# Turning x1 for the GRU from 32x32 blocks on VectorE, and loading the other relations' weights one by one

## What is computed

```python
x = _layernorm(x + _L0_gnn_ref(x, adj, W, a_src, a_dst))        # graph attention, 4 heads -> x1
def _L1_gnn_ref(x, adj, weight, w_ih, w_hh, b_ih, b_hh):
    A = (adj != 0).astype(x.dtype)
    h = x                                                       # first state = x1
    for i in range(3):
        m = jnp.einsum('bnd,de->bne', h, weight[i])
        aggr = jnp.einsum('bst,bsd->btd', A, m)
        h = _gru_cell(aggr, h, w_ih, w_hh, b_ih, b_hh)
    return h
x = _layernorm(x + _L1_gnn_ref(x, adj, ...))                    # -> x2
x = _layernorm(x + _L2_gnn_ref(x, adj, ...))                    # 4 relations; adj holds only 0 and 1 here
x = _layernorm(x + _L3_gnn_ref(x, adj, W, a))                   # graph attention, 1 head
```

## Time and profile before

| | |
|---|---|
| runs (3) | median 2617.78 us, 2617.44 to 2618.26 |
| profiled execution, first to last instruction | 2616.2 us |
| busy: PE / PEld / DVE / ACT / POOL | 98% / 85% / 79% / 62% / 42% |
| granted TensorE clock, mean | 0.992 |
| data moved by DMA | 128.99 MB, 265105 packets, 49 GB/s |
| packets under 512 B | 139760 |

### The profile page before, as it was taken

One profiled execution on the slowest core, in us unless ns is written; L12 is line 12 of the kernel. 1 busy time (PEld: TensorE's weight loads), 2 busy tenths in 40 slices (PEclk: granted clock), 3 DMA queues, 4 the chain that ended last, 5 costly groups with the idle time before them and its releaser, 6 DMA issues.

```text
span 2616.2 us, 48544 instructions
## 1 busy us (share of the span) xinstructions
PE 2564.6 (98%) x14979; PEld 2219.6 (85%) x14979; DVE 2064.6 (79%) x5210; ACT 1629.9 (62%) x4153; POOL 1093.8 (42%) x1264
## 2 busy tenths in 40 slices
PE   7999999999999999999999999999999999999995
PEld 6888888888888888888888888888888888888884
DVE  7877887877887877887877887877887877887765
ACT  5556665666665666665666665666665666665553
POOL 1333444443444443444443444443444443444342
PEclk9999999999999999999999999999999999999997
DMA  5212121112121212111212121212121212121000
GB/s 166 78 39 54 33 52 46 52 50 58 32 53 44 54 50 58 32 53 43 54 50 58 31 54 42 55 50 58 31 54 42 55 49 58 31 55 38 27 13 21
DMA packets 265105, 128.99 MB, mean 49 GB/s; under 512 B 139760, under 2 KB 249840, under 8 KB 264816
## 3 DMA queue, kind: packets, MB, share of 16 engines
q1 hardware_dynamic: 245120, 107.97, 15.8%
q10 hardware_dynamic: 19696, 17.44, 2.0%
HBM read 108.27 MB, written 17.08 MB: 48 GB/s over the span
## 4 chain that ended last, share of the span: by engine, by line
PE 94%; DVE 1%; issue 1%; ACT 0%; POOL 0%; POOLq 0%; DVEq 0%; ACTq 0%
PE psum L938 60%; PE psum L792 10%; PE psum L926 6%; PE psum L853 6%; PE psum L975 3%; PE psum L842 3%; PE psum L869 2%; PE psum L811 1%; PE psum L913 1%; PE psum L861 1%; DVE stats L1351 0%; ACT x L1176 0%; POOL rstd L1508 0%; DVE first_scores L1322 0%; DVE moments L1355 0%
## 5 line engine op out<-in xcount | busy, mean ns | idle before, releaser
L938 PE MATMUL psum<-ag_h,wc_h 128*128 128x512 f32 (+1 forms) x1188 | 489.0, 412 | 2.7 <-issue 2.0
L938 PE MATMUL psum<-ht_h,whh_h 128*128 128x512 f32 (+1 forms) x1188 | 483.0, 407 | 0.7 <-ACT g_z L1159 0.6
L938 PE MATMUL psum<-ht_h,whh_l 128*128 128x512 f32 (+1 forms) x1188 | 462.8, 390 | 0.0
L938 PE MATMUL psum<-ag_l,wc_h 128*128 128x512 f32 (+1 forms) x1188 | 461.9, 389 | 0.0
L938 PE MATMUL psum<-ht_l,whh_h 128*128 128x512 f32 (+1 forms) x1188 | 461.7, 389 | 0.0
L938 PE MATMUL psum<-ag_h,wc_l 128*128 128x512 f32 (+1 forms) x1188 | 461.5, 388 | 0.0
L1506 POOL TENSOR_SCALAR rstd<-moments 128x2 f32<-128x2 f32 x256 | 73.3, 286 | 858.6 <-DVE moments L1355 854.1
L1557 POOL TENSOR_TENSOR ht<-ht,g_n 128x512 f32<-128x512 f32 (+1 forms) x198 | 251.7, 1271 | 71.3 <-ACT g_n L1164 63.7
L938 PEld LDWEIGHTS psum<-ht_h,whh_l 128*128 128x128 f32 x1188 | 224.9, 189 | 50.8
L938 PEld LDWEIGHTS psum<-ag_h,wc_l 128*128 128x128 f32 x1188 | 223.4, 188 | 50.5
L938 PEld LDWEIGHTS psum<-ht_l,whh_h 128*128 128x128 f32 x1188 | 225.7, 190 | 40.0
(11 more groups left out here) (152 smaller groups left out, 6218.3 us busy)
## 6 DMA issues: line engine op xcount, KB each, us to landing
first_scores<-first_kept SPq DMA_DIRECT2D x116, 256.0 KB, 3.7
adj_i<-in_adj_dram SPq DMA_DIRECT2D x128, 128.0 KB, 3.2
x_in<-in_x_dram SPq DMA_DIRECT2D x64, 256.0 KB, 3.8
out_dram<-out_t ACTq DMA_DIRECT2D x64, 256.0 KB, 2.5
x_blocks<-in_x_dram SPq DMA_DIRECT2D x464, 32.0 KB, 2.1
part<-in_adj_dram SPq DMA_DIRECT2D x32, 256.0 KB, 3.3
adj_g<-in_adj_dram SPq DMA_DIRECT2D x31, 256.0 KB, 3.3
last_scores<-last_kept SPq DMA_DIRECT2D x59, 128.0 KB, 3.0
```

Of the source, the lines that this page charges most:

```text
L938: last = mm(dst, s, m, start=(first and k == 0), stop=(last_part and k == len(flat) - 1))
```

## The change

Units from 5 on (halves 3 to 32) no longer use `gru_turn0`. SP writes x1 of the unit to a DRAM scratch (`x1_keep`), waits for its landing, reads it back in 32x32 blocks (`x1_blocks`, 4 DMAs of 512 pieces of 128 bytes; the blocked loads of x take the same new form), DVE transposes the blocks into `ht` (`x1_turn`), ACT rounds to `ht_h`, and DVE writes `ht_l` (`x1_low`). No bank of LIGHT is taken. The DVE transpose waits until both `gru_fin` steps of half k-2 have been through PE. The weights of further relations are no longer loaded at the start, but one by one by SP under the branch.

```diff
 SLOTS: "xs": 2 -> "xs": 4
-gru_agg(0,1,0)
-gru_agg(0,1,1)  att_pv(pre,1,1)  att_exp(pre,1,1)  gru_new(-1,2,1)  att_res(pre,1,1)
+gru_agg(0,1,0)  x1_keep(1,0)
+gru_agg(0,1,1)  x1_blocks(1,0)  att_pv(pre,1,1)  att_exp(pre,1,1)  gru_new(-1,2,1)  att_res(pre,1,1)
 gru_hn(0,1,0)
-gru_rzh(0,1,0)  gru_fin(-1,0)  att_norm(pre,1,1)  rel_bias(-1,0)
-gru_r(0,1,0)
-gru_z(0,1,0)  att_scores(post,-2,1,0)  rel_adjt(-1,0)  rel_mask(-1,0)
+gru_rzh(0,1,0)  gru_fin(-1,0)  att_norm(pre,1,1)  rel_bias(-1,0)  x1_keep(1,1)
+gru_r(0,1,0)  x1_turn(1,0)
+gru_z(0,1,0)  x1_blocks(1,1)  x1_low(1,0)  att_scores(post,-2,1,0)  rel_adjt(-1,0)  rel_mask(-1,0)
 gru_in(0,1,0)  gru_fin(-1,1)  gru_norm(-1,0)  att_prob(post,-2,1)  post_load(-1,1)
-gru_hn(0,1,1)  gru_turn0(1,0)
+gru_hn(0,1,1)
 gru_rzh(0,1,1)  att_xt(pre,2,0)  gru_n(0,1,0)  rel_h1(-1,0)  x_blocks(2,1)  rel_bias(-1,1)  att_norm(post,-2,0)
-        gru_new(0,1,0)  att_pt(post,-2,1,0)
-gru_r(0,1,1)  att_wh(pre,2,0,0)  att_wh(pre,2,0,1)  att_rows(pre,2,0)  rel_y1(-1,0)  gru_norm(-1,1)  gru_turn0(1,1)
+        gru_new(0,1,0)  att_pt(post,-2,1,0)  x1_turn(1,1)
+gru_r(0,1,1)  att_wh(pre,2,0,0)  att_wh(pre,2,0,1)  att_rows(pre,2,0)  rel_y1(-1,0)  gru_norm(-1,1)  x1_low(1,1)
         rel_rest(-1,0)
...
 SP:
+            def load_blocks(i, blocks):
+                for f in range(P // TURN):
+                    sp.dma_start(xs[i][f * TURN:(f + 1) * TURN].rearrange("i c (m j) -> i c m j", j=TURN),
+                                 blocks[f].rearrange("i c g b j -> i c (g b) j")).then_inc(s_xs[i], 16)
+            def x1_keep(u):
+                sp.wait_ge(s_x1, u + 1)
+                if u - 2 >= X1_BLOCKED:
+                    sp.wait_ge(s_ht0, u)
+                at = 2 * place_of(u)
+                sp.dma_start(x1_kept[u % 2].rearrange("g n d -> n g d"), x1[half_of(u) % 3][:, at:at + 2, :]).then_inc(s_x1_kept, 16)
+            def x1_blocks(u):
+                i = take(sp, "xs", "x1_blocks", u)
+                sp.wait_ge(s_x1_kept, 16 * (u - X1_BLOCKED + 1))
+                load_blocks(i, x1_kept[u % 2].rearrange("g (b i) (c f j) -> f i c g b j", i=TURN, f=P // TURN, j=TURN))
-                sp.dma_start(wrs[:], L2_gnn_weight[1:R].rearrange("r (c p) o -> p r c o", p=P)).then_inc(s_rest, 16)
+            def rel_rest(u):
+                with sp.If(any_other > 0):
+                    for r in range(2, R + 1):
+                        after(sp, s_yr_ps, (R - 1) * u + r - 2)
+                        sp.dma_start(wr_other[:], L2_gnn_weight[r - 1].rearrange("(c p) o -> p c o", p=P)).then_inc(s_wr, 16)
...
 ACT:
+            def x1_turn(u):
+                k = half_of(u)
+                act.wait_ge(s_ht0, u + 2)
+                f(ht_h[k % 2][:, :, unit_columns(u)], ht[k % 2][:, :, unit_columns(u)], ACT.Copy).then_inc(s_ht0_h, 1)
...
 DVE:
+            def x1_turn(u):
+                k = half_of(u)
+                i, rounds = ring("xs", "x1_blocks", u)
+                dve.wait_ge(s_fin_ps, 2 * k - 3)
+                dve.wait_ge(s_xs[i], 64 * (rounds + 1))
+                stand(dve)
+                nc.vector.transpose(ht[k % 2][:, :, unit_columns(u)], xs[i][:]).then_inc(s_ht0, 1)
+            def x1_low(u):
+                k = half_of(u)
+                dve.wait_ge(s_ht0_h, u + 2)
+                tt(ht_l[k % 2][:, :, unit_columns(u)], ht[k % 2][:, :, unit_columns(u)],
+                   ht_h[k % 2][:, :, unit_columns(u)].bitcast(F32), ALU.subtract).then_inc(s_ht0_l, 1)
```

More of the change, by code:

```diff
@@ L42 @@
     "att_xt": ("xt",), "x_blocks": ("xs",), "att_direct": ("light",),
-    "att_pt": ("light",), "att_pv": ("light",),
+    "x1_blocks": ("xs",), "att_pt": ("light",), "att_pv": ("light",),
     "rel_adjt": ("light", "adjt"), "rel_bias": ("x2s",), "rel_mask": ("mt",),
@@ L290, in placed @@
     if name == "x_blocks" and not blocked("pre", u):
+        return []
+    if name in ("x1_keep", "x1_blocks", "x1_turn", "x1_low") and u < X1_BLOCKED:
         return []
@@ L398, in bass_gnn_stack @@
         xt_h, xt_l = sb("xt_h", [P, C, 2 * P], F32R), sb("xt_l", [P, C, 2 * P], F32R)
-        wh = [sb(f"wh{i}", [P, 2, D + 2 * H0]) for i in range(2)]
+        wh = [sb(f"wh{i}", [P, 2, D + 2 * H0]) for i in range(SLOTS["wh"])]
         stats = [sb(f"stats{i}", [P, 2, 6]) for i in range(4)]
@@ L418, in bass_gnn_stack @@
         Y_OF = {"pre": 0, "post": 1}
+        x1_kept = [nc.dram_tensor(f"x1_kept{i}", (2, P, D), F32, kind="Internal").ap() for i in range(2)]
+        s_x1_kept = sem("x1_kept_landed")
         class Layer:
@@ L463, in bass_gnn_stack @@
         s_x = [sem(f"x_loaded{i}") for i in range(2)]
-        s_xs, s_xturned = [sem(f"x_blocks_loaded{i}") for i in range(2)], sem("x_turned")
+        s_xs, s_xturned = [sem(f"x_blocks_loaded{i}") for i in range(SLOTS["xs"])], sem("x_turned")
         s_adj = [sem(f"adj_loaded{i}") for i in range(2)]
@@ L671, in pre_load @@
                 sp.dma_start(x_in[i][:], x[2 * u:2 * u + 2].rearrange("g n d -> n g d")).then_inc(s_x[i], 16)
+            def load_blocks(i, blocks):
[12 more added lines that the diff above has]
+                load_blocks(i, x1_kept[u % 2].rearrange("g (b i) (c f j) -> f i c g b j", i=TURN, f=P // TURN, j=TURN))
             def x_blocks(u):
                 i = take(sp, "xs", "x_blocks", u)
[L675 to L678, removed]
+                load_blocks(i, x[2 * u:2 * u + 2].rearrange("g (b i) (c f j) -> f i c g b j", i=TURN, f=P // TURN, j=TURN))
             def gru_load(k):
@@ L945, in gru_hn @@
                         pe.wait_ge(s_prep_lo, len(PIECES))
-                    pe.wait_ge(s_ht0_l, 2 * k + 2)
+                    pe.wait_ge(s_ht0_l, 2 * k + (2 if k < half_of(X1_BLOCKED) else len(units(k))))
                 else:
@@ L1195, in _ @@
                        "rel_adjt": rel_adjt, "rel_h1": rel_h1, "rel_rest": rel_rest,
-                       "gru_turn0": gru_turn0, "gru_agg": gru_agg, "gru_hn": gru_hn, "gru_r": gru_r, "gru_z": gru_z,
+                       "x1_turn": x1_turn, "gru_turn0": gru_turn0, "gru_agg": gru_agg, "gru_hn": gru_hn, "gru_r": gru_r, "gru_z": gru_z,
                        "gru_n": gru_n, "gru_turn": gru_turn, "rel_norm": rel_norm, "gru_norm": gru_norm})
@@ L1468, in _ @@
                        "att_res": att_res, "att_norm": att_norm, "rel_h1": rel_h1, "rel_y1": rel_y1,
-                       "rel_rest": rel_rest, "gru_turn0": gru_turn0,
+                       "rel_rest": rel_rest, "x1_turn": x1_turn, "x1_low": x1_low, "gru_turn0": gru_turn0,
                        "gru_agg": gru_agg, "gru_z": gru_z, "gru_in": gru_in, "gru_new": gru_new, "gru_split": gru_split,
```

30 lines of the change are left out of this document (20 added, 10 removed).

## The result

The changed kernel takes **2795.68 us** (median of 4 runs, 2793.32 to 2796.65) against 2618.02 us for the kernel before beside it (2617.44 to 2622.21). The ratio is 1.0676, with an interval of 1.0661 to 1.0691: slower by 6.8%. The forecast was 2753 us, with a range of 2660 to 2805. Its direction and both stops were right; it was 43 us short. The forecast's own range for the case of two stops, 2725 to 2790, does not hold the measured time; the wide range does, because it also took in most of the rival "the blocks land late" (2782 to 2817).

The account below looks back on a forecast made before the run. PE was taken as the bound, never waiting. Two new stops, less the transposes shed, cost 4.6 us in each of 29 halves (133.4), plus 2.0 and 1.6 on 2616.2: 2753 us, range 2660 to 2805.

Parts of the forecast that it names:

- the case of two stops: PE stands before `rel_h1` and again before `att_pv`: 3.9 to 5.8 us a half, 2725 to 2790 us; chance 0.66.
- the blocks land late: Rival: scratch blocks reach DVE's first turn 1 to 2.2 us later, shifting everything behind: 2782 to 2817 us; chance 0.12.
- The bound and the gain: PE never waits and sets the time; removing 236 transposes at 0.44 us per four saves 26.0 us.
- Which stop comes first, and who stands behind the wait: DVE's first turn waits, holding ACT, then POOL's mask; PE stands 2.46 us before `rel_h1`.
- What ends the wait: PE's transposes of `gru_fin(-1,1)`, done at 1307.34, release DVE's first turn; the blocks' landing is hidden.
- I take the early half: Of block landings between 1306.1 and 1309.6 the early half was taken; the late end adds 2.2 us.
- The second stop: PE stands 3.0 us before `att_pv` for the bank freed by ACT's `wh` copy; both stops make 4.6 us a half.
- PE alone sets the rest of the half.: Behind `att_pv` PE has its old work, helpers at most some 1.5 us later; nothing is made good or added.
- The other edits: Relation weights: one load fewer at the start, an untaken SP branch per unit; -2 to +1 us, taken as nothing.
- The sum: 29 halves x 4.6 = 133.4, plus 2.0 for half 32, on 2616.2, plus 1.6: 2753 us, 5.2% slower.
- PE only sheds its work: Rival: the mask is ready when PE comes, so only the 26.0 us go: 2592 us; chance 0.09.
- only the first stop holds: Rival: POOL or DVE makes up time, so the bank for `att_pv` is free: +46, 2664 us; chance 0.09.

Follow-up runs that it names:

- e9: Changed kernel with the first turn behind the `wh` copies, the second at the half's end, SP's second-unit store and loads behind `post_load(-1,1)`: 2594.11 us, 0.9913 of before.
- e5: e3 with PE turning both units of the finished half back in the half's first `gru_fin`: 2728.48 us, ratio 1.0423 to before.
- e6: e3 with SP's store of the first unit (`x1_keep(1,0)`) issued one line earlier: 2713.53 us, ratio 1.0366 to before.
- e4: Changed kernel with 23 identity transposes on PE put in each of the two stops, results overwritten: 2774.2 us, ratio 1.0599 to before.
- e7: Changed kernel without the scratch path: PE's `gru_turn0` as before, but one-by-one relation weights and four-DMA input blocks kept: 2616.41 us, ratio 0.9993 to before.
- e3: Changed kernel with only the second turn of a half moved, behind the `wh` copies: 2728.61 us, ratio 1.0423 to before.

## Why the prediction was right, and where its sum was short

- **The bound and the gain.** Right. PE alone set the time, and of its 26.0 us all but 2.6 came back in e9, where nothing waits.
- **Which stop comes first, and who stands behind the wait.** Right on the place and on the queues: DVE stands before the transpose, ACT behind DVE, POOL's `rel_bias` and mask behind ACT, and PE before `rel_h1`, released by POOL's mask. The stop was forecast at 2.46 us and is 2.65 (79.4 / 30). From the transpose's start to `rel_h1` the sum had 1313.84 - 1307.45 = 6.39 us; the rows above have 1312.75 - 1306.43 = 6.32.
- **What ends the wait.** Wrong: the forecast had PE end it, and the landing did in all 30 halves. The term that failed is the way through DRAM ("I take the early half"), and it makes 0.74 us a half (21 us). The store went 7.34 us ahead of the end of PE's transposes by the forecast and 7.14 in the trace. The forecast then counted 2.5 (landing of the store) + 1.5 (three issues more) + 2.1 (landing) = 6.1 us; the chain shows 3.28 + 2.02 + 2.33, and with the hand-overs 1306.43 - 1298.62 = 7.81. The largest miss is the store's landing, 0.8 us, for which the forecast gave no bounds; the issues are 0.5 more, the blocks' landing 0.2 and the hand-overs 0.2. The issues (bounds 1.5 and 2.9) and the blocks' landing (2.1 and 4.2) did fall nearer their early ends. The rival "the blocks land late" named the view that decides this, and that view decided for it. Its price of 1 to 2.2 us a half was too high for the 0.74 found, so that the measured time lies inside its 2782 to 2817 only because the clock, which it did not count, added about as much. e5 and e6 show which wait is last, and e6 that with the other one the forecast's 6.50 us hold. The Trainium skill, DMA: Bandwidth & Descriptors, Specifications, had been quoted for pieces under 512 bytes running below line rate. No run here shows whether that bears on the landing, for all the loads of blocks have pieces of 128 bytes: 64 KB of them land in 2.4 us, 32 KB in 2.1.
- **The second stop.** Right in cause and releaser: ACT's `wh` copy behind the second turn. Its end was forecast 8.41 us behind `rel_h1` and came at 8.41 in 10 of 27 halves and at about 8.17 in the others; that it meets the forecast exactly is chance. The forecast's path ran over POOL's L1614, and that is the path in the halves with 8.17 us. In the 10 others the clock is low while `rel_h1` runs, its result comes late, and DVE is still at the two L1406 on `out_t` when L1614 is done (the rows above: 1316.13 + 1.52 = 1317.65 against 1315.88 + 1.30 = 1317.18); the sum had neither. PE's idle time there is 1.9 us a time (48.5 / 26), not 3.0, mostly because its own work between the stops ran at half clock in many halves, so that PE came later. Idle time and lost time are two things here.
- **"PE alone sets the rest of the half."** Right on the waits, wrong on the pace, because the sum had no term for the clock. Between 180 and 2480 us the clock falls to 0.5 for 3.4 us 27 times, once in each half. In 16 of them it falls between 0.7 us before and 1.3 us behind the start of `rel_h1`. The work slowed there lies ahead of the second stop, which waits for ACT and swallows the loss but for 0.24 us (8.41 against 8.17). In the other 11 it falls some 9 us behind `rel_h1`, on work of the third part, and that part is then 69.9 instead of 68.33 us. That is 0.66 us a half in the third part and, against e4, 0.09 in the second, 22 us in all; e4 puts it at 21.5 us in the kernel's whole time. The other 0.13 us of the third part stays in e4 (68.34 against the forecast's 68.21), so it isn't the clock; its cause is open. No rival had the clock either.
- **The other edits.** Right: e7 shows no cost.
- **The sum.** 2753 + 29 x (0.74 + 0.79 - 0.16) = 2793; measured 2795.7. The table above was made from the same trace, so this shows where the time is, and e4, e5 and e6 show why. One step of the forecast's arithmetic does not close: 3.9 to 5.8 us a half give 2733 to 2788, not 2725 to 2790.
- **The rival "PE only sheds its work"** was set at 2592. It is not this kernel, whose mask came 2.65 us too late, but another placing of the same steps reaches it: e9.
- **The rival "only the first stop holds"** did not come true here. e3 makes its case and takes 2728.6 us, not 2664, for the reasons given there.

Still open: why the store lands in 3.1 us in its place and in 2.1 one line earlier. In its place SP issues it 0.45 us behind the load of `last_scores` (1298.17 and 1298.62), and the DMA share is 0.45 from 1300 to 1306 us; but no kernel took the neighbouring transfers away.

## What to carry to other kernels

Work taken from the bounding engine pays only where the step that replaces it is placed behind everything that the bounding engine needs next; here the same instructions cost 178 us in one place, nothing in a second and gain 23 in a third, since the second place only moved the stop. Where an instruction waits for two things, moving one of them may show nothing (0 and 15 us) while both together give 125; ask the trace which of them comes last, and sum both to the end with their late bounds. When an engine that never waited is made to wait, put in a term for its clock as well.
